# A selective-scan mixer: dt projections in pairs one chunk ahead, a ring of twelve state buffers, other steps for the side work

## The chip, the cores and the metric

One core of one Trainium2 chip. The metric is device time in microseconds, the median of several runs; lower is better. The core has five engines that run their own instruction streams and meet only through semaphores: PE (TensorE, matmuls and transposes), DVE (VectorE, here above all the scans), ACT (ScalarE, functions and copies), POOL (GpSimd, elementwise products) and SP, which issues most of the DMA transfers.

## The reference

The program computes a state space mixer (Mamba) on images of 384 channels and 32 x 32 positions, batch 8, and then some further layers. Only the mixer is touched. For each image of L = 1,024 positions, with 768 inner channels d and 16 states n:

```python
xz = xseq @ in_proj_w.T;  xin, z = split(xz)
u  = silu(depthwise_conv3(xin) + conv_b)
dbc = u @ x_proj_w.T                      # 24 columns dt, 16 columns B, 16 columns C
dt = softplus(dbc[..., :24] @ dt_proj_w.T + dt_proj_b)
A  = -exp(A_log)
def step(h, inp):                         # for each position t in turn
    dA = exp(dt_t[..., None] * A)
    h  = dA * h + (dt_t * u_t)[..., None] * B_t[:, None, :]
    y  = einsum('bdn,bn->bd', h, C_t)
y = (ys + u * D) * silu(z)
out = y @ out_proj_w.T
```

A layer norm over channels stands before it and a residual sum behind it.

## The kernel before, in words

A chunk is half an image, 512 positions, so there are 16 chunks; `h` is the half (even chunks are first halves, h = 0). The 768 channels are 6 tiles of 128 partitions (index k). A chunk has 96 steps `q = 16 * k + n`, one for each tile and state. All five engines run through the same numbering of steps, each in its own function `scan` (PE from L591 on, ACT from L833, POOL, DVE), and the work of a step is:

- ACT computes the decay `exp(dt * A)` (`decay`, L745 into a ring buffer `slot` for the six states of `PE_N`, L754 into one of four banks of PSUM `state` for the others).
- The drive `dt * u * B` is a product of POOL into `slot` (`drive`, L957) for the ten states outside `PE_N`. For the six in `PE_N` it is made by PE into a bank of `state`: a matmul with a diagonal matrix of B (L575), or, for the two in `TURN_N`, a transpose of something that ACT has scaled (L805, L572).
- DVE runs the scan over 512 positions (`recur`, L1053), and in the odd chunk it starts from the end state of the even one, which ACT has copied away in `keep_state` (L763, even chunks only).
- The state is multiplied by C, by POOL for the nine states in `POOL_N` (L967, `POOL_LAG` = 9 steps behind POOL's own drives), by DVE for the seven others (`times_c`, L1061). The result stands in `slot`.
- PE adds the 16 products of a tile in the bank `ysum` by transposing them (`sum_state`, L457). `SUM_AT[n]` is the step, counted from the tile's first, at which that stands in PE's program. After it the buffer of `slot` is free for the step `SLOTS` = 16 later.

Around these stands the side work, and it belongs to two other chunks. For the next chunk: input projection `in_proj` (L363), convolution on DVE (`conv`, L1032 and L1034) and its silu, `x_proj` (L370) into a bank of PSUM, `copy_xp` and the store of B and C, `dt_proj` (L391), `dt_read_tile` (L724) and `softplus` (L728), the norm. For the chunk before: the output projection (L442, L445). For this chunk: `dt * u` (POOL, L946), `turn_u` and `copy_u` (its transpose for PE's drives), the gate projections (L423) and their silu (L734), `turn_y` (L512 and L516) and the gating (`gated_y`, L1067).

The order of all this is written out by hand: the constants `..._AT` give the step at which a piece stands in the program of its engine. Where several engines have a part, each has its own step: `DT_AT` for PE, `DT_READ_AT` for ACT. Side work shares three PSUM banks BX, BY, BZ (px, py, pz), and the waits on semaphores such as `dt_read`, `gated`, `u_copied` say when the bank is free. An engine that must wait holds everything behind it in its queue.

Four of the six dt projections (`EARLY` = 4) are made in the preceding chunk at PE's steps 57 to 69, the last two in the chunk itself at steps 1 and 19. The softplus of the first four tiles is at ACT's step 80 of the preceding chunk, that of the last two at step 31. ACT holds one table of functions at a time, so silu, softplus and exp each need a table load; the groups of `SILU_AT` stand together for that reason (`L734`, `L728`, `L885` are the loads' lines).

## Time and profile before

| | us |
|---|---|
| median of 3 runs | 3620.64 (3618.16 to 3621.16) |
| the profiled execution | 3612.3 |
| its span, first to last instruction | 3610.5 |
| PE busy | 3324.0 (92%) |
| DVE busy | 3191.6 (88%) |
| ACT busy | 2663.0 (74%) |
| POOL busy | 2573.6 (71%) |
| mean granted TensorE clock | 0.973 of full speed |

The mixer is the first 2,625 us or so, and the layers behind it are the rest. A row of a timeline gives the start (us from the span's start), the duration, the engine, the line and operation, out<-in with their shapes, how many instructions are merged in it (x), and in brackets how long the engine was idle before it and what ended that. A 512-column matmul in f32 is two instructions (x2), a transpose of 128 x 512 is four. Durations overlap a little with the next instruction, so the time from one start to the next is what an operation costs.

### The profile page before, as it was taken

To read this page: it belongs to the slowest core of one execution; us is meant where nothing else is said; L and a number is where in the kernel's file an instruction comes from. 1 tells how busy PE (TensorE), PEld (TensorE's weight loads), DVE (VectorE), ACT (ScalarE), POOL (GpSimd) and SP (SyncE) were. 2 spreads that over 40 slices of the span, in tenths; PEclk is the share of its full clock that TensorE was granted. 3 is DMA by queue.
4 is the path that set the end of the run, shared out by engine and by line. 5 is a ranking of instruction groups with operands and counts; after the bars stand their busy time and mean duration, and the time that the engine had idled before them with its cause. 6 is when DMAs were issued, how large, how long until landed. Compare 5 with 4: busy or idle time off the path is not lost. (4 is left out here: it accounts for less than half of the span.)

```text
span 3610.5 us, 49832 instructions
## 1 busy us (share of the span) xinstructions
PE 3324.0 (92%) x16962; PEld 2349.5 (65%) x16962; DVE 3191.6 (88%) x3280; ACT 2663.0 (74%) x5126; POOL 2573.6 (71%) x2045
## 2 busy tenths in 40 slices
PE   6999989999999999999999999998879998889997
PEld 3666666666666666666666666666657786567776
DVE  3999999999999999999999999999967887876886
ACT  4877887787878778877877887787655555875653
POOL 3899999989998998999999899999901101551100
PEclk7999999999999999999999999999999999999998
DMA  4020211202020220202021120202210123650212
GB/s 145 2 94 21 93 54 50 86 18 86 19 103 28 77 86 19 86 19 102 22 83 69 35 86 19 94 10 94 70 45 35 54 84 119 252 193 18 71 37 88
DMA packets 83585, 249.88 MB, mean 69 GB/s; under 512 B 15213, under 2 KB 24045, under 8 KB 73093
## 3 DMA queue, kind: packets, MB, share of 16 engines
q1 hardware_dynamic: 82564, 245.65, 18.8%
q8 instruction: 136, 2.23, 0.3%
q10 hardware_dynamic: 768, 1.05, 0.1%
q14 instruction: 117, 0.95, 0.1%
HBM read 204.73 MB, written 41.95 MB: 68 GB/s over the span
## 5 line engine op out<-in xcount | busy, mean ns | idle before, releaser
L957 POOL TENSOR_TENSOR slot<-dtu,b_rep 128x512 f32<-128x512 f32 x960 | 1214.7, 1280 | 106.6 <-PE ysum L457 106.5
L967 POOL TENSOR_TENSOR slot<-slot,c_rep 128x512 f32<-128x512 f32 x864 | 1099.5, 1278 | 65.4 <-ACT carry L763 57.5
L754 ACT ACTIVATE state<-dt,aneg 128x512 f32<-128x512 f32 x960 | 656.9, 689 | 248.4 <-DVE slot L1061 177.0
L457 PE MATMUL ysum<-ident,slot 128*128 128x128 f32 x6144 | 808.7, 277 | 17.1 <-POOL slot L967 16.9
L457 PEld LDWEIGHTS ysum<-ident,slot 128*128 128x128 f32 x6144 | 713.5, 144 | 156.8 <-issue 134.0
L1053 DVE TENSOR_TENSOR_SCAN slot<-state,slot 128x512 f32<-128x512 f32 x384 | 456.1, 1204 | 57.7 <-ACT state L754 57.7
L1053 DVE TENSOR_TENSOR_SCAN slot<-state,carry,slot 128x512 f32<-128x512 f32 x384 | 478.2, 1264 | 0.0
L575 PE MATMUL state<-diag_b,dtu_t 128*128 128x128 f32 x3072 | 420.6, 281 | 54.5 <-ACT carry L763 41.3
L575 PEld LDWEIGHTS state<-diag_b,dtu_t 128*128 128x128 f32 x3072 | 383.3, 194 | 129.4 <-issue 128.7
L1061 DVE TENSOR_TENSOR slot<-state,c_rep 128x512 f32<-128x512 f32 x672 | 447.2, 667 | 0.0
L745 ACT ACTIVATE slot<-dt,aneg 128x512 f32<-128x512 f32 x576 | 404.6, 711 | 2.8 <-PE ysum L457 2.7
L1053 DVE TENSOR_TENSOR_SCAN state<-slot,carry,state 128x512 f32<-128x512 f32 x240 | 301.4, 1271 | 31.2 <-PE state L575 16.1
L1053 DVE TENSOR_TENSOR_SCAN state<-slot,state 128x512 f32<-128x512 f32 x240 | 289.5, 1215 | 33.9 <-PE state L575 22.9
L1616 ACT ACTIVATE hid<-ph_l,bias_l 128x512 f32<-128x512 f32 x240 | 165.0, 691 | 202.6 <-PE ph_l L1427 201.3
L805 ACT ACTIVATE dbu_t<-dtu_t,b_t 128x128 f32<-128x128 f32 x768 | 243.0, 389 | 0.0
L1427 PE MATMUL ph_l<-xh,w 128*128 128x512 f32 x720 | 215.4, 409 | 27.0 <-DVE xl L1845 10.8
L1427 PE MATMUL ph_l<-xl,w 128*128 128x512 f32 x720 | 208.5, 399 | 0.0
L1849 DVE TENSOR_REDUCE big_l<-hid 128x1 f32<-128x1024 f32 x120 | 144.1, 1214 | 69.9 <-ACT hid L1616 69.8
L2155 POOL TENSOR_TENSOR xsum<-xn_l 128x1024 f32<-128x1024 f32 x8 | 21.7, 2718 | 255.2 <-DMA xn_l<-between_layers 255.2
L1438 PE MATMUL acc_l<-gh,w 128*128 128x512 f32 x720 | 193.9, 405 | 7.5 <-ACT y L1643 7.5
L572 PE MATMUL state<-ident,dbu_t 128*128 128x128 f32 x768 | 123.4, 286 | 74.1 <-ACT carry L763 38.4
L1631 ACT ACTIVATE g<-hid,gain_l 128x1024 f32<-128x1024 f32 x120 | 135.3, 1149 | 67.1 <-DVE gl L1858 33.8
(268 smaller groups left out, 5925.8 us busy)
## 6 DMA issues: line engine op xcount, KB each, us to landing
c_rep<-rows_of_b_and_c SPq DMA_DIRECT2D x64, 1024.0 KB, 4.7
xres_l<-between_layers SPq DMA_DIRECT2D x18, 1536.0 KB, 10.0
xn_l<-between_layers SPq DMA_DIRECT2D x13, 1536.0 KB, 6.4
...
```

Of the source, the lines that this page charges most:

```text
L457: last = mm(ysum[:, cols], slot[:, (NS * k + n) % SLOTS, cols], ident[:], start=first and j == 0, stop=final, is_transpose=True, skip_grou ...
L575: last = mm(state[:, q % BANKS, cols], dtu_t[:, cols], diag_b[:, diag_n().index(n), cols], start=True, stop=True)
L745: af(slot[:, q % SLOTS], dt[:, k], ACT.Exp, scale=aneg[:, k, n:n + 1]).then_inc(exp_done, 1)
L754: af(state[:, (NS * k + n) % BANKS], dt[:, k], ACT.Exp, scale=aneg[:, k, n:n + 1]).then_inc(exp_done, 1)
L805: last = af(dbu_t[:, at % SCALED, cols], dtu_t[:, cols], ACT.Copy, scale=b_t[:, h, j, n:n + 1])
L957: tt(slot[:, q % SLOTS], dtu[:, k % 2], b_rep[:, b_row(n)], ALU.mult).then_inc(dbu_done, 1)
L967: tt(slot[:, q % SLOTS], slot[:, q % SLOTS], c_rep[:, n], ALU.mult).then_inc(pool_mult_done, 1)
L1053: v.tensor_tensor_scan(to, decay, drive, carry[:, q:q + 1] if h else 0.0, ALU.mult, ALU.add).then_inc(scan_done, 1)
L1061: v.tensor_tensor(slot[:, q % SLOTS], state[:, q % BANKS], c_rep[:, n], ALU.mult).then_inc(mult_done, 1)
L1427: last = mm(ph[h][:], w1[:, t, m * P:(m + 1) * P], src[f // FFN_B][:, t, half(h)], start=p == 0 and t == 0, stop=p == 1 and t == CT - 1)
L1438: last = mm(acc[HALVES * m + h][:], w2[:, k, m * P:(m + 1) * P], src[f // FFN_B][:, k % AHEAD, half(h)], start=k == 0 and p == 0, stop=k = ...
L1616: af(hid[:, m, half(h)], ph[h][:], ACT.Identity, bias=bias1[:, f // FFN_B, m:m + 1]).then_inc(up_read, 1)
```

## The change

- `SLOTS` goes from 16 to 12, and POOL's products come 5 steps behind its drives instead of 9. POOL multiplies the states 0, 1, 3, 4, 5, 7, 9, 10, 11 instead of 0, 1, 2, 4, 5, 8, 9, 10, 12; DVE the other seven.
- All six dt projections of a chunk are made in the preceding chunk. `x_proj` writes the 24 dt rows twice, at partitions 0 to 23 and 64 to 87, and the weights `w_dt` stand at both places too, so the two projections of a pair take their operands from different partitions and write to different banks.
- The tiles 4 and 5 of `dt` have two places, by the parity of the chunk (`dt_tile`), since the current chunk still uses its own. All six tiles go through softplus at ACT's step 80, in two instructions.
- The x projection's six matmuls stand at steps 52, 52, 53, 53, 53, 54 instead of all at 54.
- Many other constants of steps are new, as the diff shows. `IN_STEP` and `GATE_STEP` are all zero, so an input or gate projection stays in one piece.

```diff
-SLOTS = 16
+SLOTS = 12
 BANKS = 4
 BX, BY, BZ = 0, 1, 2
 XROWS, XBC = 64, 32
+DT_ROWS = (0, 64)
+XALL = 88
 GROUP = 4
-POOL_N, POOL_LAG = (0, 1, 2, 4, 5, 8, 9, 10, 12), 9
-PE_N, TURN_N, SCALE_AHEAD, SCALED = (5, 7, 11, 13, 14, 15), (11, 13), 5, 2
-SUM_AT = (3, 4, 8, 6, 11, 11, 8, 12, 13, 14, 13, 14, 15, 16, 14, 16)
-
-COPY_Y, TURN_Y_AT, GATED_Y_AT = 5, (29, 38, 50, 73, 81, 1), (35, 41, 53, 75, 84, 2)
+POOL_N, POOL_LAG = (0, 1, 3, 4, 5, 7, 9, 10, 11), 5
+PE_N, TURN_N, SCALE_AHEAD, SCALED = (5, 7, 11, 13, 14, 15), (11, 13), 6, 2
+SUM_AT = (5, 3, 6, 4, 11, 11, 8, 12, 13, 13, 16, 14, 16, 16, 14, 16)
+
+COPY_Y, TURN_Y_AT, GATED_Y_AT = 5, (29, 37, 55, 73, 81, 1), (33, 41, 60, 77, 88, 2)
 Y_IN = (BX, BZ, BY, BX, BX, BZ)
-OUT_AT, OUT_PER = (0, 4, 12), (3, 3, 1)
-OUT_IN, RES_AT = (BX, BY, BX), (14, 23, 23)
+OUT_AT, OUT_PER = (0, 6, 12), (3, 3, 1)
+OUT_IN, RES_AT = (BX, BY, BX), (8, 22, 23)
 LAST_OUT_IN, EARLY_OUT_AT, LATE_OUT_AT = (BX, BY, BZ), (88, 82, 84), (89, 90, 91)
 X_SUM_AT = 86
-MEAN_AT, CENTER_AT, SQUARE_AT, VAR_AT, RSTD_AT, SCALE_AT = 75, 87, 91, 88, 94, 95
+MEAN_AT, CENTER_AT, SQUARE_AT, VAR_AT, RSTD_AT, SCALE_AT = 75, 79, 90, 91, 95, 95
 FIRST_NORM_AT = (18, 21, 25, 25, 31, 28)
-GATE_AT, GATE_IN = (19, 25, 37, 49, 68, 72), (BX, BZ, BY, BX, BY, BZ)
-IN_AT, IN_IN = (27, 32, 36, 39, 44, 48), (BY, BZ, BX, BX, BY, BZ)
-CONV_IN_AT, CONV_AT = (32, 39, 41, 46, 50, 54), (32, 37, 40, 44, 49, 51)
-SILU_AT = (31, 45, 57, 80)
+GATE_AT, GATE_IN = (19, 24, 36, 51, 72, 74), (BX, BZ, BY, BX, BY, BZ)
+IN_AT, IN_IN = (28, 32, 33, 39, 43, 50), (BY, BZ, BX, BX, BY, BZ)
+CONV_IN_AT, CONV_AT = (34, 38, 39, 46, 49, 55), (32, 37, 38, 48, 50, 52)
+SILU_AT = (31, 43, 57, 80)
 SILU_CONV, SILU_GATE = ((), (0, 1, 2), (3, 4, 5), ()), ((0, 1), (2,), (3,), (4, 5))
-SOFT = ((4, 6), (), (), (0, 4))
-XP_AT, XP_COPY_AT = 54, 60
-DT_AT, DT_IN = (57, 60, 64, 69, 1, 19), (BX, BY, BZ, BX, BZ, BZ)
-DT_READ_AT = (62, 65, 75, 76, 8, 26)
-EARLY = 4
-DT_U_AT = 13
-TURN_U_AT, COPY_U_AT = (91, 8, 28, 45, 61, 78), (95, 20, 33, 50, 67, 83)
-TURN_B_AT, COPY_B_AT = 80, 87
-DIAG_AT = (1, 93, 1, 9, 5, 12)
-HALO_AT = 15
+SOFT_AT = 3
+IN_STEP, GATE_STEP, XP_STEP = (0, 0, 0), (0, 0, 0), (-1, -1, 0, 0, 0, 1)
+XP_AT, XP_COPY_AT = 53, 62
+DT_AT, DT_IN = (59, 61, 65), (BX, BY, BX, BY, BX, BY)
+DT_READ_AT = (64, 65, 66, 66, 73, 75)
+DT_U_AT = 4
+TURN_U_AT, COPY_U_AT = (87, 14, 31, 41, 60, 75), (95, 19, 35, 49, 68, 84)
+TURN_B_AT, COPY_B_AT = 83, 91
+DIAG_AT = (94, 0, 6, 23, 12, 6)
+HALO_AT = 32
...
+def dt_tile(c, k):
+    return k if k < GROUP else k + 2 * (c % 2)
+
...
+def b_runs(j):
+    rows, runs = b_rows(j), []
+    while rows:
+        by = rows[1] - rows[0] if len(rows) > 1 else 1
+        n = 1
+        while n < len(rows) and rows[n] - rows[n - 1] == by:
+            n += 1
+        runs.append((rows[0], by, n))
+        rows = rows[n:]
+    return runs
...
-        w_x = sb("w_x", [P, KT, XROWS])
-        w_dt = sb("w_dt", [DTR, DI])
+        w_x = sb("w_x", [P, KT, XALL])
+        w_dt = sb("w_dt", [XALL, DI])
...
-        dt = sb("dt", [P, KT, T])
+        dt = sb("dt", [P, KT + 2, T])
...
-            sp.dma_start(w_x[:, :, XBC:], xw[:, :, DTR:]).then_inc(x_w_in, 16)
-            sp.dma_start(w_x[:, :, 0:DTR], xw[:, :, 0:DTR]).then_inc(x_w_in, 16)
-            sp.dma_start(w_dt[:], dt_wT).then_inc(dt_w_in, 16)
+            sp.dma_start(w_x[:, :, XBC:XROWS], xw[:, :, DTR:]).then_inc(x_w_in, 16)
+            for row in DT_ROWS:
+                sp.dma_start(w_x[:, :, row:row + DTR], xw[:, :, 0:DTR]).then_inc(x_w_in, 16)
+                sp.dma_start(w_dt[row:row + DTR], dt_wT).then_inc(dt_w_in, 16)
...
+            def x_proj(d, h, ks=range(KT)):
+                for k in ks:
+                    if k == 0:
+                        pe.wait_ge(conv_done, KT * (d + 1))
                     pe.wait_ge(u_done, KT * d + k + 1)
-                    last = mm(pz[0:XROWS, :], w_x[:, k], u[h][:, k], start=k == 0, stop=k == KT - 1)
-                last.then_inc(xp_full, 1)
+                    last = mm(pz[0:XALL, :], w_x[:, k], u[h][:, k], start=k == 0, stop=k == KT - 1)
...
+            def dt_proj(d, pair):
+                if pair == 0:
                     pe.wait_ge(xp_read, d + 1)
                     if later(d):
                         pe.wait_ge(z_read, KT * (d - 1) + 4)
-                if m == 1 and later(d):
-                    pe.wait_ge(gated, KT * (d - 1) + 3)
-                if m == 2 and later(d):
-                    pe.wait_ge(u_copied, KT * (d - 1) + 5)
-                if m == 3:
-                    pe.wait_ge(dt_read, KT * d + 1)
-                if m == 4:
-                    if later(d):
-                        pe.wait_ge(gated, KT * d)
-                    else:
-                        pe.wait_ge(u_copied, 1)
-                if m == 5:
-                    pe.wait_ge(u_copied, KT * d + 2)
-                mm(pg[DT_IN[m]][:], w_dt[:, m * P:(m + 1) * P], xp[0:DTR, :], start=True, stop=True).then_inc(dt_full, 1)
+                        pe.wait_ge(gated, KT * (d - 1) + 3)
+                else:
+                    pe.wait_ge(dt_read, KT * d + 2 * pair)
+                for m in (2 * pair, 2 * pair + 1):
+                    rows = slice(DT_ROWS[m % 2], DT_ROWS[m % 2] + DTR)
+                    mm(pg[DT_IN[m]][:], w_dt[rows, m * P:(m + 1) * P], xp[rows, :], start=True, stop=True).then_inc(dt_full, 1)
...
                     if later(c):
                         pe.wait_ge(res_done, CT * c)
                     else:
-                        pe.wait_ge(dt_read, EARLY)
-                if k == 1:
-                    pe.wait_ge(dt_read, KT * c + 6)
-                if k == 2:
+                        pe.wait_ge(dt_read, KT)
+                if t == 0 and k == 1:
+                    pe.wait_ge(u_copied, KT * c + 2)
...
-                if k == 4:
+                if t == 0 and k == 4:
                     if more:
-                        pe.wait_ge(dt_read, KT * (c + 1) + 2)
+                        pe.wait_ge(dt_read, KT * (c + 1) + 6)
...
-                af(dt[:, m], pg[DT_IN[m]][:], ACT.Identity, bias=dtb[:, m:m + 1]).then_inc(dt_read, 1)
-
-            def softplus(d, first, end):
-                act.wait_ge(dt_read, KT * d + end)
-                af(dt[:, first:end], dt[:, first:end], ACT.Softplus).then_inc(dt_done, end - first)
+                af(dt[:, dt_tile(d, m)], pg[DT_IN[m]][:], ACT.Identity, bias=dtb[:, m:m + 1]).then_inc(dt_read, 1)
+
+            def softplus(d):
+                act.wait_ge(dt_read, KT * (d + 1))
+                for tiles in (slice(0, GROUP), slice(dt_tile(d, GROUP), dt_tile(d, KT - 1) + 1)):
+                    af(dt[:, tiles], dt[:, tiles], ACT.Softplus).then_inc(dt_done, tiles.stop - tiles.start)
...
                 if k == 1:
-                    pe.wait_ge(dt_read, KT * c + 5)
+                    if later(c):
+                        pe.wait_ge(gated, KT * c)
+                    else:
+                        pe.wait_ge(u_copied, 1)
...
-                        if q == DT_AT[k] and (after or k >= EARLY):
-                            dt_proj(d if k < EARLY else c, k)
-                        if q == GATE_AT[k]:
-                            gate_proj(c, h, k)
-                        if after and q == IN_AT[k]:
-                            in_proj(d, 1 - h, k)
+                        for t in range(CT):
+                            if q == GATE_AT[k] + GATE_STEP[t]:
+                                gate_proj(c, h, k, t)
+                            if after and q == IN_AT[k] + IN_STEP[t]:
+                                in_proj(d, 1 - h, k, (t,))
+                    for pair in range(KT // 2):
...
-                    if after and q == XP_AT:
-                        x_proj(d, 1 - h)
+                    for k in range(KT):
+                        if after and q == XP_AT + XP_STEP[k]:
+                            x_proj(d, 1 - h, (k,))
...
```

The waits of the turned u and y and of the gate projections follow the new use of the banks. `b_runs` splits the load of B rows into evenly spaced runs; with this `PE_N` each group has one run, as before.

## Rows read from the trace of the kernel before

**Rows 1.** The page's part 1, busy time of each engine.

```profile
PE 3324.0 (92%) x16962; PEld 2349.5 (65%) x16962; DVE 3191.6 (88%) x3280; ACT 2663.0 (74%) x5126; POOL 2573.6 (71%) x2045
```

**Rows 2.** Stretches: chunk 8, chunk 9 (us, busy us of each engine, clock, DMA).

```profile
1349.68:1510.75 161.07, 149.43 (x838) 102.47 (x837) 148.90 (x159) 136.24 (x322) 147.72 (x124) 1.00 0.16 57
1510.75:1669.17 158.42, 150.49 (x842) 104.52 (x841) 153.97 (x159) 122.00 (x225) 149.74 (x122) 0.98 0.16 60
```

**Rows 3.** Timeline of DVE in chunk 8, the rows behind its longer waits.

```profile
1354.85 0.69 DVE L1067 TENSOR_TENSOR u<-pz,gate 128x512 f32<-128x512 f32 x1 [0.61 <-PE pz L516]
...
1356.58 0.67 DVE L1061 TENSOR_TENSOR slot<-state,c_rep 128x512 f32<-128x512 f32 x1
...
1357.17 1.21 DVE L1053 TENSOR_TENSOR_SCAN slot<-slot,state 128x512 f32<-128x512 f32 x1
...
1360.93 1.23 DVE L1053 TENSOR_TENSOR_SCAN state<-slot,state 128x512 f32<-128x512 f32 x1 [1.43 <-PE state L575]
...
1368.25 1.23 DVE L1053 TENSOR_TENSOR_SCAN state<-slot,state 128x512 f32<-128x512 f32 x1 [1.56 <-PE state L572]
...
1401.41 1.22 DVE L1053 TENSOR_TENSOR_SCAN slot<-state,slot 128x512 f32<-128x512 f32 x1 [2.66 <-ACT state L754]
...
1426.79 0.75 DVE L1032 SCALAR_TENSOR_TENSOR acc<-px,cw,acc 128x511 f32<-128x511 f32 x1 [0.91 <-ACT acc L702]
...
1477.74 0.69 DVE L1067 TENSOR_TENSOR u<-px,gate 128x512 f32<-128x512 f32 x1 [1.37 <-PE px L516]
...
1485.92 2.34 DVE L1053 TENSOR_TENSOR_SCAN slot<-state,slot 128x512 f32<-128x512 f32 x2 [1.24 <-ACT state L754]
```

**Rows 4.** Timeline of DVE in chunk 9, the same.

```profile
1515.81 0.69 DVE L1067 TENSOR_TENSOR u<-pz,gate 128x512 f32<-128x512 f32 x1 [0.25 <-PE pz L516]
...
1521.89 1.29 DVE L1053 TENSOR_TENSOR_SCAN state<-slot,carry,state 128x512 f32<-128x512 f32 x1 [1.25 <-PE state L575]
...
1529.21 1.29 DVE L1053 TENSOR_TENSOR_SCAN state<-slot,carry,state 128x512 f32<-128x512 f32 x1 [1.32 <-PE state L572]
...
1635.49 0.69 DVE L1067 TENSOR_TENSOR u<-px,gate 128x512 f32<-128x512 f32 x1 [0.70 <-PE px L516]
```

**Rows 5.** Timeline of PE at the start of chunk 8.

```profile
1352.38 1.13 PE L575 MATMUL state<-diag_b,dtu_t 128*128 128x128 f32 x8 [0.28 <-ACT carry L763]
...
1356.46 1.12 PE L391 MATMUL pz<-xp,w_dt 24*128 24x512 f32 x2
...
1357.51 1.12 PE L442 MATMUL px<-u,w_out 128*128 128x512 f32 x2
...
1359.77 1.06 PE L575 MATMUL state<-diag_b,dtu_t 128*128 128x128 f32 x8
...
1361.10 5.32 PE L442 MATMUL py<-u,w_out 128*128 128x512 f32 x12
...
1367.54 0.60 PE L572 MATMUL state<-ident,dbu_t 128*128 128x128 f32 x4
```

**Rows 6.** Timeline of ACT in chunk 8, steps 31 and 80.

```profile
1394.33 1.28 ACT L734 ACT_TABLE_LOAD   x1
...
1398.02 1.06 ACT L728 ACTIVATE dt<-dt 128x1024 f32<-128x1024 f32 x1
...
1481.77 1.91 ACT L728 ACTIVATE dt<-dt 128x2048 f32<-128x2048 f32 x1
```

**Rows 7.** Groups of PE, 720 to 1360 us (count, busy us, mean ns, idle).

```profile
L391 PE MATMUL pz<-xp,w_dt 24*128 24x512 f32 x24 | 13.4, 640 | 0.8 <-ACT dtu_t L774 0.8
...
L363 PE MATMUL py<-xn,w_in 128*128 128x512 f32 x48 | 21.9, 592 | 0.0
```

**Rows 8.** Waits of POOL, 720 to 1360 us (total, times, longest).

```profile
POOL slot L957 <- PE ysum L457: 28.5, 11, 4.0
```

**Rows 9.** Timeline: DVE at the start of chunk 0, POOL in chunk 15.

```profile
69.89 3.45 DVE L1053 TENSOR_TENSOR_SCAN slot<-state,slot 128x512 f32<-128x512 f32 x3 [22.82 <-ACT state L754]
...
2596.14 2.41 POOL L974 TENSOR_TENSOR dt<-xn_l 128x1024 f32<-128x1024 f32 x1
```

More of the change, by code:

```diff
@@ L339, in norm_var, with in_proj @@
                 last.then_inc(var_full, 1)
-            def in_proj(d, h, m):
-                if m == 0:
+            def in_proj(d, h, m, ts=range(CT)):
+                if 0 in ts and m == 0:
                     pe.wait_ge(normed, d + 1)
@@ L639, in _ @@
                 in_proj(0, 0, m)
-            pe.wait_ge(x_w_in, 32)
+            pe.wait_ge(x_w_in, 48)
             pe.wait_ge(gap_set, 1)
             x_proj(0, 0)
-            pe.wait_ge(dt_w_in, 16)
-            for m in range(EARLY):
-                dt_proj(0, m)
+            pe.wait_ge(dt_w_in, 32)
+            for pair in range(KT // 2):
+                dt_proj(0, pair)
             turn_b(0)
@@ L903, in _ @@
             store_bc(0, 0)
-            for m in range(EARLY):
+            for m in range(KT):
                 dt_read_tile(0, m)
-            softplus(0, 0, EARLY)
+            softplus(0)
             nc.scalar.preload_act_table_set("natural_log_exp_and_others")
```

74 lines of the change are left out of this document (36 added, 38 removed).

## The prediction

> **What bounds the kernel now.** I read the page's shares first: PE 92%, DVE 88%, ACT 74%, POOL 71% of the span [rows 1]. A share over the span cannot say which engine sets the pace in the mixer (16 chunks of 96 steps, the first 2,625 us), so the stretch table comes next. Chunk 8 (even: it keeps its end states) lasts 161.07 us with DVE busy 148.90, PE 149.43, POOL 147.72; chunk 9 (odd) lasts 158.42 with 153.97, 150.49, 149.74 [rows 2]. Three engines are equally near full. The scans follow each other on DVE, so a chunk is DVE's work plus DVE's idle time: 12.2 us in chunk 8, 4.5 us in chunk 9. Where it idles, DVE's timeline tells [rows 3, 4]; chunks 1 to 14 repeat these gaps at the same steps, even or odd. In us, even/odd:
> - gating of the last y at step 2: 0.61/0.25, on PE
> - scan 7: 1.43/1.25, scan 11: 1.56/1.32, on PE's drives
> - scan 32: 2.66 and 0.16 right behind it/0, on ACT
> - convolution at step 44: 0.91/0, on ACT
> - gating at step 75: 1.37/0.70, on PE
> - scan 81: 1.24/0, on ACT
> - five short ones at steps 23, 30, 51, 58, 62, of which only the sum matters: 2.0/0, which with the others makes 11.9 of the 12.2.
> What the change saves elsewhere is worth nothing unless one of these gets shorter.
>
> **The change, part by part.**
>
> *Scans 7 and 11.* From its drive of scan 5 at 1352.38 to that of scan 11 PE has no gap [rows 5]: the turned y, two matmuls of an output projection, one dt projection (1356.46 to 1357.51: 1.05 us), the last two matmuls, a sum, drive 7 at 1359.77, a sum, the seven matmuls of the next output projection in one go (from 1361.10 on), a sum, drive 11 at 1367.54. The dt projection leaves, so drive 7 comes 1.05 us earlier: at most 0.4/0.2 of that stall is left, I take 0.2/0.1. The output projection moves from steps 4 and 5 to 6 and 7, and drive 11 comes between its halves: four matmuls less before it (0.9 each: six of the twelve instructions, and the last two), two sums more (0.44 each), 2.8 us less. The stall of scan 11 goes.
> What is late next are drives 13 and 14, behind that second half. From the start of drive 5 PE has 1.0 (drive) + 1.3 (y) + 3.6 + 0.4 (sum) + 0.9 (drive 7) + 1.3 (three sums) + 2.7 + 0.4 (drive 11) + 3.6 + 0.4 (sum) + 0.4 (drive 13) = 16.0. DVE starts scan 5 at 4.8 (1357.17 less 1352.38), and with eight scans at 1.13 (2.34 for two in a row), two multiplies at 0.59 (1356.58 to 1357.17) and the 0.2 it stands ready for scan 13 at 15.2 [rows 3]. I charge 1.0/0.9; nothing to 2 are the bounds.
>
> *Scan 32.* At step 31 ACT makes three table loads at 1.28, two silu at 0.57 and a softplus of 1.06: 6.0 us [rows 6]. Softplus and one load go, 2.3 us. The carry of step 27, for which ACT waits before the block, comes some 1.2 us sooner, as state 11 is now multiplied by POOL. Together more than 2.82: the stall goes.
>
> *Scan 81.* The block at step 80 is 3 x 1.28 + 2 x 0.57 + 1.91 = 6.9 us [rows 6]; the softplus of tiles 4 and 5 comes to it, 8.0. It also starts later, since state 12 is now multiplied by DVE. On the other side DVE's centering of x moves from step 87 to 79 and lies beside the block. Net nothing in even chunks (1.2 stays), 0.8 new in odd ones; bounds 0 and 2.4.
>
> *Scan 44.* The block of three conv silu and a gate silu, 2 x 1.28 + 4 x 0.57 = 4.9, moves from step 45 to 43, and the convolution that lay beside it from 44 to 48. ACT has 1.4 of exps and carries around the block; DVE has four scans and a multiply, 5.1. New stall 1.3/0.3, bounds 0 and 2.2. The convolution's own 0.91 goes: its input copy keeps step 46, and it now comes two steps later instead of two earlier. Of the short waits, 1.2/0 stays.
>
> *Steps 75 to 79.* The turned y waited for the fourth read of dt at ACT's step 76, which is now at 66, and the gating comes two steps later: 1.37/0.70 goes. But gate projections 4 and 5 (2.7 each) now stand at PE's steps 72 and 74, the first behind the read of dt tile 5 at ACT's 75. From the end of scan 71 to the end of drive 79 I count 11.7 us for PE and 10.8 for DVE: 0.9/0.5, bounds 0 and 2.
>
> *The pairs.* A dt projection is two matmul instructions; 24 of them took 13.4 us, 0.56 each, against 0.46 of a full one (21.9 for 48) [rows 7]. No row shows matmuls in two different row ranges of the array, so a pair costs between 1.1 us (all beside each other) and 2.2 (all in a row). I take 1.6: the two instructions of a tile stay in order, the middle two meet. That is 1.9 us less PE per chunk; the time gets only what the stretches above count. The Trainium skill (TensorE: Matmul & The Clock Gate, on packing small matmuls) says that matmuls in distinct row groups run concurrently, starts some 4 ns apart. By that a pair would be 1.1 us and PE would save 3.3 us per chunk; no row here shows it, and no term above would change.
>
> *The x projection* is the same six matmuls around one drive, its 88 columns for 64 at the same 512 moving ones: 0 to 0.2 per chunk, I take 0. SP's queue has the same loads per chunk; its waits for POOL's products end earlier with the shorter lag.
>
> *Twelve buffers* are the price. POOL has 120 large operations a chunk at 1.23 us, 24.8 per 16 steps [rows 2]; DVE has 16 scans and 7 multiplies, 22.0 (odd: 23.0), and is slower than POOL only where convolutions (1.35), gating and the two passes over x stand, at steps 32 to 60 and 79 to 95. So over steps 0 to 31 POOL loses up to 2.8 us per 16 steps and lives on its lead. That lead was 9 steps at most and is now 5, about 7 us, and a buffer must be summed by PE 12 steps after its drive, not 16. POOL already waits 28.5 us in four chunks for such sums, 7.1 each [rows 8]. Now its drive of step 16 needs the sum of state 4, which PE makes between drives 14 and 15, about 17.5 us after the start of drive 5. From there on POOL goes without a pause and meets DVE at scans 25, 26 and 28, with 0.4, 0.7 and 0.2 missing; 0.8 more may come at scan 23, whose drive stands in PE's queue behind a sum that needs POOL's product. I take 1.3/0.3, bounds 0 and 2.1.
>
> *Once each.* Ahead of the first scan, two more dt projections with their reads, 1.5 each (an estimate from the 1.05 of a projection and the read that follows it), and the softplus of 1.06: +4.1. In the last chunk POOL's sum over x, 2.41 and as much again [rows 9], meets a shorter lead: +1.5, between 0 and 4.7. The layers behind the mixer stay as they are.
>
> **The sum.** Even: 0.6 (step 2) + 0.2 + 1.0 + 1.3 (POOL) + 1.3 + 1.2 + 0.9 + 1.2 = 7.7 for 11.9. Odd: 0.2 + 0.1 + 0.9 + 0.3 + 0.3 + 0.5 + 0.8 = 3.1 for 3.5. Eight even chunks at -4.2 and seven odd ones at -0.4 (the last has no next chunk) make -36.4; with +5.6 it is -30.8. The profiled execution took 3612.3 us, so 3581.5; the median of the runs lies 8.3 above it, thus **3590**, 0.8% less.
>
> **Rivals.**
> *A, the stalls just go.* PE reaches drives 13 and 79 in time, ACT scan 44, POOL keeps its lead. What stays is 0.6 + 1.2 + 1.2 in an even chunk and 1.0 in an odd one: 8 x -8.9 and 7 x -2.5, -88.7 + 5.6, thus 3538. For it: PE is behind most stalls and gets room. Against: with 148 to 154 us of work on three engines, a period of 155 leaves little for them to miss each other.
> *B, the idle time only changes its step.* The pairs run in a row, the longer block costs 2.4, scans 13 and 44 twice what I charge: 3621, give or take 7.
> *C, slower: POOL sets the pace.* The mechanism is the ring of twelve: drive, scan, product, sum, drive. If POOL never regains its lead, each 16 steps last as long as the slower of the two: even 24.8 + 24.8 + 27.2 + 26.6 + 24.8 + 24.8 = 153 where DVE alone has 147, odd 156 for 153. On top of the stalls without POOL's (6.4 and 2.8) that makes 12.4 and 5.8 idle, 18.2 for 15.4: +22 over the mixer, +6 at the ends, 3649. It decides once POOL must idle more than its present 9 to 13 us a chunk [rows 2]. For it: POOL's waits for sums. Against: DVE never waited for POOL in chunks 1 to 14, and steps 32 to 60 give POOL some 4 us back.
>
> **How the numbers follow.** Forecast 0.45 (its own range 3570 to 3611), A 0.15, B 0.12, C 0.28. The runs of the kernel agree within 0.1%; 0.2%, 7 us, is about what can be told from no change. Faster 0.6 (forecast and A), same 0.12, slower 0.28. The range goes from near A's time to C's, 3545 to 3650.
>
> **What would show it.** In the trace after: no DVE wait on PE at scan 11, none on ACT at scan 32; nine table loads a chunk, not ten; DVE waits with POOL as releaser at steps 22 to 30; a pair of about 1.6 us; the first scan at 74 us, not 69.9 [rows 9]; periods near 157 and 158. Wrong if DVE's waits on POOL pass 3 us a chunk (then C), or if an even chunk lasts under 153 us (then A).

## The result, and the profile after

The changed kernel took 3627.86 us (median of 15 runs, 3626.29 to 3632.18) against 3618.84 us for the kernel before, ratio 1.0027 [1.0019, 1.0034]: slower by 0.27%, where 0.8% less was forecast. The profiled executions lie further apart, 3631.7 and 3612.3, 19.4 us: 4.9 ahead of the first scan, 9.9 from the first scan of chunk 0 to that of chunk 15 (2398.7 before, 2408.6 after), 4.6 from there to the end.

Part 1 of the page, to be read beside [rows 1]: the busy time of PE fell by 34 us and that of ACT by 10, those of DVE and POOL stayed.

```profile
PE 3289.6 (91%) x16962; PEld 2345.2 (65%) x16962; DVE 3193.1 (88%) x3280; ACT 2652.8 (73%) x5110; POOL 2573.0 (71%) x2045
```

Stretches of the changed kernel, chunk 8, chunk 9 and three pieces of 4 us around step 79 of chunk 8 (columns as in [rows 2]; the third figure from the end is the granted clock). The even chunk is as long as before. The odd one is 2.3 us longer, at the same busy DVE. In the middle one of the three DVE and POOL nearly stop while PE works through the mean of x at a granted clock of 0.61.

```profile
1361.20:1522.10 160.90, 149.04 (x840) 104.08 (x839) 149.25 (x159) 135.16 (x321) 148.55 (x125) 0.98 0.17 57
1522.10:1682.86 160.76, 148.71 (x841) 104.16 (x840) 153.87 (x159) 122.10 (x225) 148.59 (x121) 0.98 0.17 61
1488.00:1492.00 4.00, 1.70 (x14) 1.47 (x13) 2.96 (x4) 3.99 (x3) 4.00 (x4) 0.97 0.63 197
1492.00:1496.00 4.00, 4.00 (x6) 1.49 (x6) 0.56 (x1) 3.87 (x9) 0.70 (x1) 0.61 0.00 0
1496.00:1500.00 4.00, 4.00 (x38) 3.96 (x37) 3.76 (x3) 2.12 (x5) 3.27 (x3) 1.00 0.25 55
```

DVE's timeline in chunk 8 of the changed kernel, in the order of scans 7, 13, 23, 33, 44, 71 and 79, and the centering of the next x. [Rows 3] is its counterpart.

```profile
1371.21 1.22 DVE L1071 TENSOR_TENSOR_SCAN slot<-slot,state 128x512 f32<-128x512 f32 x1 [0.78 <-ACT state L772]
...
1379.84 1.23 DVE L1071 TENSOR_TENSOR_SCAN state<-slot,state 128x512 f32<-128x512 f32 x1 [0.64 <-PE state L586]
...
1395.34 1.22 DVE L1071 TENSOR_TENSOR_SCAN slot<-slot,state 128x512 f32<-128x512 f32 x1 [0.94 <-PE state L589]
...
1410.57 1.22 DVE L1071 TENSOR_TENSOR_SCAN slot<-state,slot 128x512 f32<-128x512 f32 x1 [0.21 <-POOL slot L975]
...
1430.68 1.23 DVE L1071 TENSOR_TENSOR_SCAN state<-state,slot 128x512 f32<-128x512 f32 x1 [0.38 <-ACT state L772]
...
1474.70 1.22 DVE L1071 TENSOR_TENSOR_SCAN slot<-slot,state 128x512 f32<-128x512 f32 x1 [0.57 <-PE state L589]
...
1489.04 1.23 DVE L1071 TENSOR_TENSOR_SCAN state<-slot,state 128x512 f32<-128x512 f32 x1 [1.94 <-PE state L589]
...
1496.24 1.75 DVE L1041 TENSOR_TENSOR xn<-xn,py 128x1536 f32<-128x1536 f32 x1 [3.68 <-PE py L351]
```

The same place in chunk 9, beside [rows 4]: the waits at scan 79 and at the centering are there too, and before there was none at either.

```profile
1649.37 1.29 DVE L1071 TENSOR_TENSOR_SCAN state<-slot,carry,state 128x512 f32<-128x512 f32 x1 [1.30 <-PE state L589]
...
1656.54 1.75 DVE L1041 TENSOR_TENSOR xn<-xn,py 128x1536 f32<-128x1536 f32 x1 [3.53 <-PE py L351]
```

So the gaps that the change was to remove at scans 11, 32 and step 75 are gone, and a new one stands at the centering in each of chunks 0 to 13, even and odd (behind them there is no further x to load). It is 3.1 to 3.8 us long in eleven of these chunks and 2.0 to 2.3 in chunks 6, 10 and 13, 46 us in all. It names PE, which made the mean of x (L351) late. Why it was late stands in three views of chunk 8: PE's timeline (gate projection 5 at 1484.43, the mean at 1491.67), that of SP's queue (the issue of the load of the next x at 1487.20), and the view of the tile `xn` over the same stretch, which has the time from issue to landing.

```profile
1484.43 2.74 PE L433 MATMUL pz<-xn,w_in 128*128 128x512 f32 x6
...
1491.67 4.54 PE L351 MATMUL py<-xn,mean_w 128*128 128x512 f32 x6 [2.30 <-DMA xn<-in_x]
```

```profile
1487.20 0.37 SPq L262 DMA_DIRECT2D xn<-in_x  x1
```

```profile
DMA to landing us min/median/max: 4.4/4.4/4.4
```

`load_x` waits for `z_full`, KT * (c + 1) of them, that is for the last gate projection of the chunk: x of chunk c + 2 goes into the half of `xn` from which the gates are projected. The gate projection moved from PE's step 72 to 74, and the load moved with it. Nothing moved PE's mean, which stays at step 75. In the kernel before, PE's timeline and SP's have these rows at that place. The load is issued at 1476.00 and lands 4.3 us later, and 4.39 us after the issue the mean starts without a wait. The margin was nil, and in six other chunks it was already less: there the mean waited 0.17 to 0.25 us for the load, as in chunk 6 (the last of the three fences).

```profile
1473.23 2.74 PE L423 MATMUL pz<-xn,w_in 128*128 128x512 f32 x6
...
1480.39 2.84 PE L332 MATMUL py<-xn,mean_w 128*128 128x512 f32 x6
```

```profile
1476.00 0.37 SPq L243 DMA_DIRECT2D xn<-in_x  x1
```

```profile
1161.68 2.84 PE L332 MATMUL py<-xn,mean_w 128*128 128x512 f32 x6 [0.17 <-DMA xn<-in_x]
```

Waits of the changed kernel over four chunks, 720 to 1360 us (total, times, longest): PE's wait for x and DVE's for the mean come once in each of them.

```profile
POOL slot L975 <- PE ysum L468: 36.6, 20, 4.0
...
DVE xn L1041 <- PE py L351: 12.7, 4, 3.6
...
PE py L351 <- DMA xn<-in_x: 9.2, 4, 2.3
```

What DVE waits at the centering has two parts. PE's own wait for x is 2.2 to 2.7 us in every one of the fourteen chunks. In eleven of them the mean then ran slowly, in 4.2 to 4.5 us, and DVE waited 3.1 to 3.8. In chunks 6, 10 and 13 it ran in 2.84 us at a clock of 1.00, and DVE waited 2.0 to 2.3. So the late load costs DVE some 2.1 us in a chunk by itself, and the fallen clock some 1.5 more where it fell. PE's row and the stretch of the mean in chunk 6:

```profile
1172.13 2.84 PE L351 MATMUL py<-xn,mean_w 128*128 128x512 f32 x6 [2.31 <-DMA xn<-in_x]
```

```profile
1172.13:1174.90 2.77, 2.77 (x7) 1.28 (x8) 0.88 (x2) 2.68 (x5) 1.02 (x1) 1.00 0.00 0
```

### The profile page after: what moved, and what is told of

Read it like the earlier page. It is cut to its first block and busy times, and to the rows that moved or that the text cites. A ratio compares the mean times of both kernels' runs of the same rounds, so it can differ in the third digit from the quotient of the medians.

```text
span 3629.9 us, 49803 instructions
## 1 busy us (share of the span) xinstructions
PE 3289.6 (91%) x16962; PEld 2345.2 (65%) x16962; DVE 3193.1 (88%) x3280; ACT 2652.8 (73%) x5110; POOL 2573.0 (71%) x2045
## 3 DMA queue, kind: packets, MB, share of 16 engines
q10 hardware_dynamic: 768, 1.05, 0.1%
## 5 line engine op out<-in xcount | busy, mean ns | idle before, releaser
L1071 DVE TENSOR_TENSOR_SCAN slot<-state,slot 128x512 f32<-128x512 f32 x288 | 346.7, 1206 | 31.1 <-ACT state L772 29.6
L1071 DVE TENSOR_TENSOR_SCAN slot<-state,carry,slot 128x512 f32<-128x512 f32 x288 | 364.1, 1266 | 2.1 <-POOL slot L975 1.2
L1071 DVE TENSOR_TENSOR_SCAN state<-state,carry,slot 128x512 f32<-128x512 f32 x192 | 243.8, 1270 | 1.0 <-POOL slot L975 1.0
L1071 DVE TENSOR_TENSOR_SCAN state<-state,slot 128x512 f32<-128x512 f32 x192 | 232.9, 1213 | 4.2 <-ACT state L772 3.2
L1071 DVE TENSOR_TENSOR_SCAN slot<-slot,state 128x512 f32<-128x512 f32 x144 | 173.4, 1204 | 31.8 <-PE state L589 22.5
L1071 DVE TENSOR_TENSOR_SCAN slot<-slot,carry,state 128x512 f32<-128x512 f32 x144 | 181.4, 1260 | 19.9 <-PE state L589 16.1
```

The costliest lines, as they stand in the source:

```text
L1071: v.tensor_tensor_scan(to, decay, drive, carry[:, q:q + 1] if h else 0.0, ALU.mult, ALU.add).then_inc(scan_done, 1)
```

## The experiments

All were timed beside the kernel before; ratios are to it. Theory: **the load of x**, as above, is what the forecast lacked. Rivals: the ring of twelve (C of the prediction), the new places of the gates and the norm for themselves, and a pair dearer than charged.

### The norm's steps and the load of x

**mean_80** and **norm_as_before**: the changed kernel with the old order of the norm, and PE's mean at step 80 or at its old step.

```diff
-MEAN_AT, CENTER_AT, SQUARE_AT, VAR_AT, RSTD_AT, SCALE_AT = 75, 79, 90, 91, 95, 95
+MEAN_AT, CENTER_AT, SQUARE_AT, VAR_AT, RSTD_AT, SCALE_AT = 80, 87, 91, 88, 94, 95   # mean_80
+MEAN_AT, CENTER_AT, SQUARE_AT, VAR_AT, RSTD_AT, SCALE_AT = 75, 87, 91, 88, 94, 95   # norm_as_before
```

> As norm_as_before, and the mean on PE at step 80 in place of 75, when x has landed. Theory L: PE no longer idles before the mean nor runs it at the lower clock (six instructions took 4.54 us in the changed kernel, 2.84 in the one before), so it gains another 5 to 20 us: 3580 to 3605, and no stretch with a granted clock near 0.6 at step 80. Theory R: no gain over the changed kernel, 3622 or more.

> The changed kernel with the steps of the norm as they were (centering at 87, square 91, variance 88, rstd 94 in place of 79, 90, 91, 95). Theory L (late x): x of the next image is loaded only when gate projection 5 is done, lands 4.4 us later, so the centering at step 79 holds DVE for 3.1 to 3.7 us a chunk. With the centering at 87 that wait is gone, but the ACT block of step 80 (8 us) is then bare and scan 81 waits about 1.8 us for it, and PE still stands 2.3 us before the mean and pushes drive 85: 0.5 to 2.5 us a chunk less, 3628 becomes 3592 to 3620. Theory R (the ring of 12 buffers costs the time): no gain, 3622 or more.

Measured: mean_80 3612.78, 0.9985 [0.9976, 0.9994]; norm_as_before 3654.45, 1.0098 [1.0084, 1.0112]. Both missed their ranges. mean_80 lies 8 us above its own, though on the load's side of the 3622 from which the ring was to decide; norm_as_before lies 34 us above its range and fell where only the ring's theory had put it. The two differ by nothing but PE's mean at step 80 or 75, and by 41.7 us. Timeline of norm_as_before, chunk 8: DVE at scans 81, 83, 86 and 87, then PE. PE idles 2.26, is slow for 4.5 (so in 7 of the 14 chunks of this run) and then makes nine sums in one go, for which POOL's buffers wait; DVE waits for POOL's drives, and PE then waits for POOL's products.

```profile
1507.79 1.22 DVE L1071 TENSOR_TENSOR_SCAN slot<-state,slot 128x512 f32<-128x512 f32 x1 [1.83 <-ACT state L772]
1511.47 1.22 DVE L1071 TENSOR_TENSOR_SCAN slot<-state,slot 128x512 f32<-128x512 f32 x1 [1.33 <-POOL slot L975]
1516.41 1.23 DVE L1071 TENSOR_TENSOR_SCAN state<-state,slot 128x512 f32<-128x512 f32 x1 [0.69 <-POOL slot L975]
1519.31 1.22 DVE L1071 TENSOR_TENSOR_SCAN slot<-slot,state 128x512 f32<-128x512 f32 x1 [1.67 <-PE state L589]
```

```profile
1505.03 4.54 PE L351 MATMUL py<-xn,mean_w 128*128 128x512 f32 x6 [2.26 <-DMA xn<-in_x]
1509.40 4.09 PE L468 MATMUL ysum<-ident,slot 128*128 128x128 f32 x36
...
1517.68 0.63 PE L468 MATMUL ysum<-ident,slot 128*128 128x128 f32 x4 [1.99 <-POOL slot L985]
```

The same place in mean_80: no wait for x and none for POOL, and the mean takes 2.74. ACT's block at step 80 is bare, as the centering no longer lies beside it.

```profile
1482.83 1.23 DVE L1071 TENSOR_TENSOR_SCAN slot<-state,slot 128x512 f32<-128x512 f32 x1 [1.84 <-ACT state L772]
```

```profile
1481.57 2.74 PE L351 MATMUL py<-xn,mean_w 128*128 128x512 f32 x6
```

**center_79_alone**: the kernel before with the changed steps of the norm, and nothing else.

```diff
-MEAN_AT, CENTER_AT, SQUARE_AT, VAR_AT, RSTD_AT, SCALE_AT = 75, 87, 91, 88, 94, 95
+MEAN_AT, CENTER_AT, SQUARE_AT, VAR_AT, RSTD_AT, SCALE_AT = 75, 79, 90, 91, 95, 95
```

> The kernel before with nothing changed but the norm's steps (centering at 79 for 87, square 90, variance 91, rstd 95). Theory L (the early centering hurts only because x is loaded late): in the kernel before the mean of x is ready at 1483.1 us where DVE comes to the centering at 1484.6 in chunk 8, and the centering lies in DVE's wait of 1.24 for scan 81: no loss, 3600 to 3622. Rival L2 (early norm steps cost by themselves, wherever x is): 3630 or more.

Measured: 3634.2, 1.0043 [1.0031, 1.0056]. The expectation for the load's theory was missed, and the rival beside it (early norm steps cost by themselves) was met. The centering itself waits for nothing here, since the gates stand early, and the 1.24 at scan 81 [rows 3] is gone. The loss is in the tail: the scaling, which waited for nothing before, waits for ACT's 1/std at the end of every chunk, 1.32 us in chunk 8 (row below) and 0.31 in chunk 9, and the gating at step 2 grows to 1.15/1.4. In the old program the new steps of the norm are a loss of 14 us.

```profile
1522.51 1.75 DVE L1027 TENSOR_TENSOR xn<-xn,py 128x1536 f32<-128x1536 f32 x1 [1.32 <-ACT py L683]
```

**no_x_load**: the changed kernel without the loads of x behind the first two, so that chunks 2 to 15 are computed from what lies in the buffer. **no_x_load_norm_as_before**: the same with the norm's old steps.

```diff
-                sp.wait_ge(z_full, KT * (c + 1))
-                sp.dma_start(xn[:, h], XV[image, :, :, h * T:(h + 1) * T]).then_inc(x_loaded[h], 16)
+                return
...
-                pe.wait_ge(x_loaded[h], 16 * (image + 1))
+                pe.wait_ge(x_loaded[h], 16)
...
```

DVE's wait for x in the centering is changed in the same way.

> The changed kernel without the loads of x for chunks 2 to 15 (each norm works on what the buffer holds, so the output is not the reference's); everything else and its order stay. Theory L (the transfer of x, issued after gate projection 5, is what PE's mean and through it the centering at 79 wait for): PE's mean starts some 2.3 us sooner and at the full clock, the centering wait of 3.6/3.3 us a chunk goes and the one at step 87 with it: 3628 becomes 3570 to 3600. Rival B2 (the transfer is only last in a row; ACT's block of step 80 ends at the same time): the wait turns into one on ACT and POOL, 3612 to 3628.

> no_x_load with the norm's steps as before (centering at 87). norm_as_before took 3654, 27 us over the changed kernel, against my expectation. If that is since PE, waiting for x at step 75, holds the sums that POOL and the drives need, it falls to 3590 to 3612 here, where nothing is waited for, and still lies over no_x_load (3581) by ACT's bare block at scan 81 (1 to 2 us a chunk). If late norm steps cost by themselves, 3625 or more.

Measured: 3580.96, 0.9897 [0.9883, 0.991], and 3610.38, 0.9976 [0.9968, 0.9985], both as expected. Without the load the change is 47 us faster, and norm_as_before 44. The new steps of the norm, a loss in the old program, are worth 29 us in the changed one once x is there. But the load brings traffic too, so the next kernel keeps it and takes away the wait alone.

**x_in_8_tiles**: x of a chunk has three tiles of 128 channels; they now go through a ring of eight tiles instead of two halves of three. Two tiles of the next x can so be loaded from the chunk's start, and the third, 256 of 768 KB, behind the last gate projection. Every byte is still loaded, and all steps are those of the change.

```diff
-        xn = sb("xn", [P, 2, CT, T])
+        xn = sb("xn", [P, XTILES, T])          # XTILES = 8; x_tile(d, t) = (CT * d + t) % XTILES
...
-                sp.wait_ge(z_full, KT * (c + 1))
-                sp.dma_start(xn[:, h], XV[image, :, :, h * T:(h + 1) * T]).then_inc(x_loaded[h], 16)
+                if later(c):
+                    sp.wait_ge(z_full, KT * c)
+                for t in range(CT):
+                    if t == CT - 1:
+                        sp.wait_ge(z_full, KT * (c + 1))
+                    sp.dma_start(xn[:, x_tile(c + 2, t)], XV[image, :, t, h * T:(h + 1) * T]).then_inc(
+                        x_loaded[h] if t == CT - 1 else x_early[h], 16)
...
```

PE waits for the third tile only before the third part of the mean. Where the three tiles of a chunk wrap around the ring, the centering, the square and the scaling are two instructions each.

> The changed kernel with x in a ring of 8 tiles of 512 columns in place of two sets of 3. Tiles 0 and 1 of the next image are loaded at the start of the chunk, into tiles that are free; only tile 2 (256 KB of 768) waits for gate projection 5. All of the traffic stays, the wait goes. Theory L (it is the wait): the mean's first two tiles are done before tile 2 lands, the centering no longer waits, 3575 to 3592 as with the loads left out (3581). Rival B3 (leaving the loads out gained by less traffic on the 16 DMA engines and memory ports): 3605 or more.

Measured: **3579.82, 0.9891 [0.9877, 0.9904]**, as expected, the best version: 1.1% under the kernel before, 1.3% under the changed one, as fast as with no load at all. Its views, one fence each: the stretches of chunks 8 and 9; DVE's timeline from step 79 on with scan 79 (even, odd), the centering and scan 81 (odd); PE's mean; SP's issue of the last tile; and the view of `xn` around it, 2.7 us to the landing.

```profile
1332.63:1489.42 156.79, 145.82 (x838) 101.77 (x837) 149.40 (x161) 134.66 (x321) 148.08 (x124) 1.00 0.16 58
1489.42:1646.66 157.24, 145.68 (x842) 102.21 (x841) 153.79 (x159) 121.89 (x226) 149.12 (x122) 1.00 0.17 62
```

```profile
1460.54 1.23 DVE L1103 TENSOR_TENSOR_SCAN state<-slot,state 128x512 f32<-128x512 f32 x1 [1.94 <-PE state L613]
...
1616.87 1.29 DVE L1103 TENSOR_TENSOR_SCAN state<-slot,carry,state 128x512 f32<-128x512 f32 x1 [1.30 <-PE state L613]
1620.42 1.74 DVE L1070 TENSOR_TENSOR xn<-xn,py 128x1536 f32<-128x1536 f32 x1
1622.59 1.28 DVE L1103 TENSOR_TENSOR_SCAN slot<-state,carry,slot 128x512 f32<-128x512 f32 x1 [0.42 <-ACT state L798]
```

```profile
1460.70 2.74 PE L375 MATMUL py<-xn,mean_w 128*128 128x512 f32 x6
```

```profile
1458.70 0.33 SPq L280 DMA_DIRECT2D xn<-in_x  x1
```

```profile
DMA to landing us min/median/max: 2.7/2.7/2.7
```

DVE's idle time is 7.0/3.2 us a chunk now, where the prediction's sum was 7.7/3.1. The same bytes, the same products, the same steps, and the wait makes 48 us. The late load of x is shown to be the cause, and its traffic is not. Of the 48 us some 17 go by the fallen clock (an estimate: eleven chunks at 1.5 us, from DVE's waits with and without it above).

### The places of the gates

**gates_early**: the changed kernel with gate projections 4 and 5 at their old places, and before them the last pair of dt projections and its reads, so the load of x is issued early enough for the mean at 75. **gates_early_norm_as_before**: the norm's old steps as well. **block_79**: gates_early with ACT's block, the centering and the gating of y tile 3 one step earlier, and the last turned u one step later.

```diff
-GATE_AT, GATE_IN = (19, 24, 36, 51, 72, 74), (BX, BZ, BY, BX, BY, BZ)
+GATE_AT, GATE_IN = (19, 24, 36, 51, 68, 72), (BX, BZ, BY, BX, BY, BZ)
-DT_AT, DT_IN = (59, 61, 65), (BX, BY, BX, BY, BX, BY)
-DT_READ_AT = (64, 65, 66, 66, 73, 75)
+DT_AT, DT_IN = (59, 61, 64), (BX, BY, BX, BY, BX, BY)
+DT_READ_AT = (64, 65, 66, 66, 68, 69)
```

> The changed kernel with gate projections 4 and 5 back at PE steps 68 and 72 (dt pair 2 at 64 for 65, its reads at ACT's 68 and 69 for 73 and 75 so that the bank is free), the norm's steps as changed. Theory L: the load of x is issued some 5 us earlier, the centering at 79 finds its mean and drive 79 is not late: both waits (3.6 and 1.9 us in an even chunk, 3.3 and 1.3 in an odd one) go or nearly go, 3628 becomes 3560 to 3595. Theory R: 3615 or more, since the ring of 12 is untouched.

> As gates_early, with the centering at 87 and the norm's other steps as before. Theory L: nothing waits for x in either, but the ACT block of step 80 is bare, so it is slower than gates_early by 0.5 to 1.7 us a chunk: 3575 to 3610. Theory R: 3615 or more.

> gates_early with the last silu and softplus block at ACT's step 79 for 80, the centering at 78 for 79, the gating of y 3 at 76 for 77, the turned u 5 at 76 for 75. In gates_early ACT stood 2.57 us idle before step 80 for the carry of step 76, with the 8 us block behind it, and scan 81 then waited. If that block is what bounds steps 80 and 81, it now starts up to 2.5 us sooner and DVE gains 0.5 to 2 us a chunk: 3575 to 3602 against gates_early's 3609. If POOL's late drives bound scan 81 (ring of 12), nothing: 3605 to 3612.

Measured: 3608.9, 0.9971 [0.9959, 0.9982]; 3635.22, 1.0043 [1.003, 1.0055]; 3629.69, 1.0028 [1.0017, 1.0038]. All three lie above the ranges expected of them. gates_early is 19 us under the changed kernel, where 33 or more were expected, since new waits took the place of part of those that went. The centering waits 0.65 instead of 3.68 and scan 79 not at all, but scan 81 now waits 1.27 for POOL and steps 69 to 71 cost 1.9/0.5 more:

```profile
1458.89 1.22 DVE L1071 TENSOR_TENSOR_SCAN slot<-slot,state 128x512 f32<-128x512 f32 x1 [0.69 <-PE state L589]
1460.81 1.23 DVE L1071 TENSOR_TENSOR_SCAN state<-state,slot 128x512 f32<-128x512 f32 x1 [0.69 <-ACT state L772]
1463.19 1.22 DVE L1071 TENSOR_TENSOR_SCAN slot<-slot,state 128x512 f32<-128x512 f32 x1 [1.15 <-PE state L589]
...
1480.31 1.76 DVE L1041 TENSOR_TENSOR xn<-xn,py 128x1536 f32<-128x1536 f32 x1 [0.65 <-PE py L351]
1483.34 1.22 DVE L1071 TENSOR_TENSOR_SCAN slot<-state,slot 128x512 f32<-128x512 f32 x1 [1.27 <-POOL slot L975]
```

With the old norm's steps the bare block costs 3.7/2.9 at scan 81, 26 us in all: the centering beside the block is worth that, once x is there. block_79 only moves the wait one step to the front (1.9 at the centering in chunk 8), and step 77 waits 1.1 for 0.5 in gates_early.

**x_in_8_tiles_gates_early** and **x_in_8_tiles_gates_70**: the ring of tiles with the gates' old places, or with `GATE_AT` 70 and 73 and the reads at 71 and 72 for the last two.

> x_in_8_tiles with gate projections 4 and 5 at steps 68 and 72 and the last two reads of dt at 68 and 69, as in gates_early. Where x is no longer late, what is left of gates_early is its own: the wait of 1.9/1.3 us at scan 79 goes, 1.3 comes at scans 69 to 71 in even chunks and 0.5 in odd ones. 3575 to 3595, within 10 us of x_in_8_tiles.

> x_in_8_tiles with the two gate projections between both: steps 70 and 73, the reads of dt at 71 and 72. Part of the wait at scan 79 goes (PE has 2.7 us less ahead of drive 79 only if it is not waiting for the read): 3565 to 3590, a few us below x_in_8_tiles if the gates' place is what makes drive 79 late, the same if it is the sum of PE's work from step 71 on.

Measured: 3607.42, 0.9967 [0.9955, 0.9979], and 3617.87, 0.9995 [0.9987, 1.0004]; both missed their expectations. Once x comes in time, the change's own places of the gates are the best of the three, by 27.6 and 38 us. The wait of 1.94/1.30 at scan 79 looked like a cost of theirs to be saved, and saving it cost more elsewhere: with the old places scan 70 waits 1.0/0.5 and the centering and scan 81 together 1.9/1.6, with 70 and 73 scan 78 alone waits 1.6/0.8.

### The ring of twelve

**ring_old_states**: the kernel before with 12 buffers and the shorter lag. **ring_alone**: also the new choice of states and the new steps of the sums.

```diff
-SLOTS = 16
+SLOTS = 12
-POOL_N, POOL_LAG = (0, 1, 2, 4, 5, 8, 9, 10, 12), 9
+POOL_N, POOL_LAG = (0, 1, 2, 4, 5, 8, 9, 10, 12), 5      # ring_old_states
+POOL_N, POOL_LAG = (0, 1, 3, 4, 5, 7, 9, 10, 11), 5      # ring_alone
...
-SUM_AT = (3, 4, 8, 6, 11, 11, 8, 12, 13, 14, 13, 14, 15, 16, 14, 16)
+SUM_AT = (5, 3, 6, 4, 11, 11, 8, 12, 13, 13, 16, 14, 16, 16, 14, 16)      # ring_alone
```

> The kernel before with 12 buffers and the lag of 5 alone, states and sum steps as they were. ring_alone with new states took 3767. If the ring itself costs that (theory R), this takes 3700 or more. If the new states without the side steps that fit them cost most of it (theory S), this takes 3625 to 3680.

> The kernel before with only the ring changed: 12 buffers, POOL 5 steps behind, the new states for POOL and the new steps of the sums. All dt work and side work stay. Theory R (the ring costs): POOL and PE wait more for each other, 3635 or more. Theory L (the ring is nearly free): 3605 to 3630, and DVE never waits over 0.5 us a chunk for POOL.

**states_as_before** and **gates_early_states**: the changed kernel, or gates_early, with the old choice of states and sums of products 0 to 3 at steps 5, 3, 8, 6.

> The changed kernel with POOL multiplying the states 0, 1, 2, 4, 5, 8, 9, 10, 12 as before (sums of state 2 at 8 and of state 3 at 6, to fit). Theory S (with state 12 on DVE, ACT's step 80 waits for a multiply and its 8 us block starts some 1.7 us later): where x is late this is hidden by the centering wait, so 3615 to 3632 here. Other places: scan 32 may wait again for up to 1 us in even chunks (the carry of step 27).

> gates_early with the same old set of states. Theory S: the wait at scan 81 (2.2/1.6 us) falls by 1 to 1.7, so 3585 to 3603 against gates_early's 3609. If the ring or PE's sums bound scan 81, nothing or slower: 3605 to 3625.

Measured: 3633.02, 1.0044 [1.0031, 1.0056]; 3766.95, 1.0412 [1.0398, 1.0427]; 3750.51, 1.0365 [1.0351, 1.0379]; 3704.05, 1.0238 [1.0224, 1.0252]. The first two are as one of their theories had it, the last two lie 118 and 79 us above the ranges expected of them. The ring and the lag alone cost the old program 14 us, so the ring has a real cost there. Its mechanism is not C's: DVE waits for POOL only at scan 74, 0.7/0, and the rest is longer waits for ACT at scan 81 (2.3 for 1.2) and for PE at scan 93 (1.2/1.9 for 0/0.7). No run has the changed program with the ring of sixteen, so what the ring costs there is not shown. The choice of states is another matter: new states in the old program cost 134 us more, old states in the changed program 123, in gates_early 95. In ring_alone the largest single wait is scan 81, on ACT; in chunk 9:

```profile
1751.21 1.28 DVE L1053 TENSOR_TENSOR_SCAN slot<-state,carry,slot 128x512 f32<-128x512 f32 x1 [3.13 <-ACT state L754]
```

The rest of the 95 to 134 us is spread over many steps, and no run tells one mechanism from another. What is shown is only that the choice of states, with the sums' steps, fits the side steps or doesn't, and that the largest numbers of this study hang on that. It stays open.

### The pair

**pair_one_row_range**: all dt projections read their 24 rows at partition 0, so the matmuls of a pair share a row range.

```diff
-                    rows = slice(DT_ROWS[m % 2], DT_ROWS[m % 2] + DTR)
+                    rows = slice(0, DTR)
```

> The changed kernel with both projections of a pair taken from partitions 0 to 23. The pair measured 1.05 us from its start to the next matmul in the changed kernel; here it should take 2.1. If PE's time counts, 3.2 us more of it a chunk make 5 to 30 us on 3628; if PE has room where the pairs stand (its steps 59 to 65), nothing: 3625 to 3632. Theory L alone says the latter.

Measured: 3633.35, 1.004 [1.0027, 1.0053], 5.5 us over the changed kernel, at the low end of what was expected if PE's time counts. PE's timeline of one pair in two row ranges (changed kernel), and of one in the same range:

```profile
1461.84 0.66 PE L405 MATMUL px<-xp,w_dt 24*128 24x512 f32 x1
1461.84 0.69 PE L405 MATMUL py<-xp,w_dt 24*128 24x512 f32 x1
...
1462.89 0.66 PE L468 MATMUL ysum<-ident,slot 128*128 128x128 f32 x4
```

```profile
1464.85 1.09 PE L405 MATMUL px<-xp,w_dt 24*128 24x512 f32 x2
1465.78 1.02 PE L405 MATMUL py<-xp,w_dt 24*128 24x512 f32 x2
```

Two instructions of one tile run beside the two of the other: 1.05 us for the pair, 1.9 in a row. The 0.85 us that each of three pairs a chunk saves, some 41 us of PE in all, are worth 5.5 us of this kernel. That is no clean price of the pairs. In the profiled executions 2.7 us of it stand ahead of the first scan (77.50 for 74.77) and 0.7 in the chunks, and in the chunks the clock helped: the mean behind the wait for x ran slowly in only 6 of 14 chunks here, for 11 in the changed kernel. What the pairs are worth where x is in time was not run.

## Why the prediction was wrong

The step that failed is **Scan 81**: "DVE's centering of x moves from step 87 to 79 and lies beside the block. Net nothing in even chunks (1.2 stays), 0.8 new in odd ones; bounds 0 and 2.4." It priced ACT's side only. The centering needs PE's mean, that needs x, and SP issues the load of x behind gate projection 5, which the change moved to PE's step 74. I counted the loads of SP's queue (the same per chunk) and POOL's products for which it waits, and never asked what each load waits for. Measured in the profile after, chunks 8 and 9: 3.7 at the centering, even, and 3.5, odd, beyond the bound of 2.4, plus 0.7/0.5 at scan 87 as PE's sums are late. With the wait taken away (x_in_8_tiles) scan 81 waits 0.2/0.4 and scan 87 0.2/0. That says too that the centering covers it better than I charged (1.2/0.8).

That one step carries the error. The profiled execution took 3631.7 us for 3581.5 forecast, 50.2 more: 0.8 ahead of the first scan (4.9 for 4.1), 46.3 in the chunks (9.9 more for 36.4 less) and 3.1 from the last chunk on (4.6 for 1.5). In chunks 8 and 9 DVE's waits add up to 10.9/6.7 for 7.7/3.1 forecast. The centering and scan 87 make 4.6/4.0 of that, where 1.2/0.8 was charged; everything else is 6.3/2.7, for 6.5/2.3. Without the wait the forecast's 3590 stands against 3580. Part of that closeness is luck, since the other terms miss by up to 1 us each, as the list shows, and cancel.

The other steps, with what the changed kernel showed (even/odd):

- *Scans 7 and 11*: right that scan 11's wait goes, 0. Scan 7 kept 0.78/0.5, for 0.2/0.1, on ACT in chunk 8. At 13 it is 0.6/0.3 for 1.0/0.9. Step 2, for which 0.6/0.2 was kept, is 0.
- *Scan 32*: right, 0 on ACT.
- *Scan 44*: 0.4/0 for 1.3/0.3. The short waits at 54 to 59 add up to 0.85, for 1.2.
- *Steps 75 to 79*: right that step 75's wait goes, and where the next comes; its size was 1.94/1.30 for 0.9/0.5, at the upper bound, and scan 71 has a new 0.6/0.
- *The pairs*: 1.05 us, the lower bound of 1.1, not my 1.6. PE saved 3.2 us a chunk, not 1.9, part of which the slow mean took back. As forecast, hardly another term moved with it. The Trainium skill (TensorE: Matmul & The Clock Gate, Part 3 on packing small matmuls), which the prediction set beside it, says that such matmuls run concurrently; this trace agrees, with starts 0 to 0.04 us apart in the pair shown above.
- *Twelve buffers*: scan 23 waits 0.9/0.65 for its drive, but the mechanism named for it is at most a small part. In chunk 8 PE works on the output projection until 1393.67 and starts the sum ahead of that drive at 1393.71, so it hardly waits for POOL's product there: PE's own work in front makes the drive late. DVE waits for POOL itself only at scan 33, 0.2/0. Together 1.1/0.65 for 1.3/0.3, so the number is near by luck. POOL's waits for sums grew from 28.5 [rows 8] to 36.6 in four chunks, and DVE's for POOL stay at 0.2 in an even chunk.
- *Once each*: the first scan at 74.8 (74 forecast), +4.9; from the last chunk on +4.6, for 1.5.
- Nine table loads a chunk: right, 36 in four chunks, for 40 before.
- *The gaps before*: that chunks 1 to 14 repeat the same gaps is not quite so. Scan 93 waited 0.69 for PE in chunk 9, and 0.75 and 1.14 in chunks 3 and 11, so chunk 9 has 4.2 where the sum has 3.5.

The first scan of the changed kernel, beside [rows 9]:

```profile
74.77 2.34 DVE L1071 TENSOR_TENSOR_SCAN slot<-state,slot 128x512 f32<-128x512 f32 x2 [26.41 <-ACT state L772]
```

Rival A fell with scans 13, 23 and 79, which stayed in every version that keeps the change's steps. Rival B comes nearest to the time, 3621, by another mechanism than it named: its longer block, dearer pairs and doubled stalls are none of them there. Its 3621 does not follow from its terms either: scans 13 and 44 doubled and 2.4 at scan 81 are 3.5 us more in an even chunk and 1.2 to 2.8 in an odd one, which from 3590 gives 3626 to 3638, the pairs not counted. Rival C was on the right side for the wrong reason: DVE's waits on POOL stayed under the 3 us from which it was to decide, even with the late x.

What the comparison does not settle is why the choice of states is worth 95 to 134 us, why gates_early gains less than its waits promised, and what the 4.6 us at the end are made of.
